# Queries and keys laid out in DRAM by head and half of the tokens: shorter rows, eight stores a group

## What is computed

```
x = x + attn_b(layernorm(x), w_qkv, w_o)

def attn_b(x, w_qkv, w_o):             # b = 16, s = 1024, hid = 256, heads = 16, d = 16
    qkv = x @ w_qkv.T * hid ** -0.5
    q, k, v = split by head            # each (b, heads, s, d)
    attn = softmax(q k^T * d ** -0.5) * (s / sqrt(s - 1))
    out = attn v * s ** -0.5
    return out @ w_o.T * hid ** -0.5
```

## Time and profile before

| what | value |
|---|---|
| median of 3 runs | 5751.51 us (5750.79 to 5752.28) |
| the profiled execution, its own time | 5750.62 us |
| its span in the profile | 5748.9 us |
| mean granted TensorE clock | 0.976 of full |
| TensorE (PE) busy | 5428.0 us, 94% of the span |
| VectorE (DVE) busy | 4498.2 us, 78% |
| ScalarE (ACT) busy | 3566.0 us, 62% |
| GpSimd (POOL) busy | 1473.5 us, 26% |
| DMA packets | 317697, 512.58 MB, mean 89 GB/s |

### The profile page before, as it was taken

One profiled execution on the slowest core, in us unless ns is written; L12 is line 12 of the kernel. 1 busy time (PEld: TensorE's weight loads), 2 busy tenths in 40 slices (PEclk: granted clock), 3 DMA queues, 4 the chain that ended last, 5 costly groups with the idle time before them and its releaser, 6 DMA issues. The chain is left out here.

```text
span 5748.9 us, 131254 instructions
## 1 busy us (share of the span) xinstructions
PE 5428.0 (94%) x50092; PEld 3660.4 (64%) x50092; DVE 4498.2 (78%) x7377; ACT 3566.0 (62%) x5406; POOL 1473.5 (26%) x1948
## 2 busy tenths in 40 slices
PE   7999668999989889999999999999999997799999
PEld 6777457999978734444444444444444444699998
DVE  7888695555557689999999999999999996755554
ACT  5777562333325458888888888888888886433332
POOL 4655453333310000111111111111111114533332
PEclk9999889999999989999999999999999998999999
DMA  2222482222229811121112111111211113222221
GB/s 74 78 84 78 137 259 77 88 93 93 89 96 333 310 56 49 58 60 57 57 59 60 57 56 60 59 57 56 60 58 57 57 54 104 75 89 93 95 86 49
DMA packets 317697, 512.58 MB, mean 89 GB/s; under 512 B 36442, under 2 KB 221156, under 8 KB 311152
## 3 DMA queue, kind: packets, MB, share of 16 engines
q1 hardware_dynamic: 291912, 441.44, 24.2%
q0 software_dynamic: 24576, 64.56, 3.5%
q10 hardware_dynamic: 808, 1.07, 0.1%
HBM read 338.59 MB, written 185.60 MB: 91 GB/s over the span
## 5 line engine op out<-in xcount | busy, mean ns | idle before, releaser
L1773 DVE TENSOR_REDUCE at_best<-at_psM 128x2 f32<-128x1024 f32 x2048 | 2430.7, 1221 | 227.5 <-PE at_psM L1830 214.3
L1729 ACT ACTIVATE at_p<-at_psE 128x1024 f32<-128x1024 f32 (+1 forms) x2688 | 2077.1, 824 | 529.5 <-PE at_psE L1846 515.7
L1846 PE MATMUL at_psE<-at_q,at_k 50*128 50x512 f32 x4096 | 1174.0, 436 | 7.5 <-ACT at_p L1729 6.3
L1830 PE MATMUL at_psM<-at_k,at_q 48*128 48x512 f32 x4096 | 1093.6, 458 | 37.5 <-DMA at_k<-scratch_qk 27.4
L1857 PE MATMUL at_psO<-at_p,at_v 128*17 128x256 f32 x16384 | 1109.9, 383 | 0.1
L1122 ACT ACTIVATE e_h_hi<-e_psH 128x512 fp32r<-128x512 f32 x512 | 306.7, 599 | 916.0 <-PE e_psH L90 864.4
L1846 PEld LDWEIGHTS at_psE<-at_q,at_k 50*128 50x128 f32 x4096 | 548.7, 185 | 462.4 <-issue 223.6
L1196 DVE SCALAR_TENSOR_TENSOR e_h_lo<-e_psH,e_h_hi 128x512 fp32r<-128x512 f32 x512 | 353.9, 691 | 595.9 <-ACT e_h_hi L1122 505.8
L1857 PEld LDWEIGHTS at_psO<-at_p,at_v 128*17 128x17 f32 x16384 | 364.1, 96 | 542.7 <-issue 345.4
L1830 PEld LDWEIGHTS at_psM<-at_k,at_q 48*128 48x128 f32 x4096 | 471.3, 185 | 312.2 <-DVE at_best L1773 147.2
L90 PE MATMUL e_psE<-e_w_hi,e_h_hi 128*128 128x256 f32 x2048 | 583.1, 285 | 0.0
(11 more groups left out here) (213 smaller groups left out, 8456.5 us busy)
## 6 DMA issues: line engine op xcount, KB each, us to landing
e_w_raw<-in_w SPq DMA_DIRECT2D x64, 1024.0 KB
scratch_qk<-cp_qkh SPq DMA_DIRECT2D x64, 512.0 KB
scratch_qk<-cp_qkl SPq DMA_DIRECT2D x64, 512.0 KB
at_q<-scratch_qk SPq DMA_DIRECT2D x256, 128.0 KB
at_k<-scratch_qk SPq DMA_DIRECT2D x252, 128.0 KB
scratch_v<-cp_va SPq DMA_DIRECT2D x32, 544.0 KB
at_v<-scratch_v SPq DMA_DIRECT2D x126, 136.0 KB, 10.0
a_x<-in_x SPq DMA_DIRECT2D x32, 512.0 KB
```

The lines of the kernel that those rows point to most:

```text
L1729: nc.scalar.activation(P[:, u:u + n, :], src, ACT.Exp, scale=HD ** -0.5).then_inc(p_ready, 1)
L1773: nc.vector.reduce_max(best[j % 2][:, h, :, qt], psM[h][:], AX_X).then_inc(m_taken, 1)
L1830: last = nc.tensor.matmul(psM[h][:, a, :], Q[j][r, 128 * qt:128 * qt + 128], K[j][r, 512 * h:512 * h + 512], start=True, stop=True)
L1846: last = nc.tensor.matmul(psE[:, u - u0 if n == 2 else 2, :], K[j][r, 128 * kc:128 * kc + 128], Q[j][r, 512 * half:512 * half + 512], star ...
```

## The change

`qk` becomes [256, 2, 4, 16, 512]: head of a batch, half of the tokens, part, feature, token of the half. The row of one head, half and feature is now 2 KB long. A load of 32 or 16 rows takes each row of its tile as two pieces of 2 KB, one from each half, and high and low parts lie next to each other, so that part and feature are one dimension. A store takes one chunk: 128 partitions of the tile go to 8 heads x 16 features. That makes eight DMAs of 256 KB a group where there were four of 512 KB, and the counts on qkv_stored go from 80 to 144 (nine DMAs of 16). Bytes, buffers and all arithmetic stay as they are.

```diff
-    qkb = qk.rearrange("r (b h) d n -> b r (h d) n", h=H)
+    qkb = qk.rearrange("(b c h) s r d n -> s b c r h d n", c=2, h=H // 2)
...
             def store_qkv(g, s, i):
-                half = slice(G * s, G * s + G)
                 sp.wait_ge(qk_lo_ready, 4 * g + 4)
                 for part in range(2):
-                    cs = slice(2 * part, 2 * part + 2)
                     for r, buf in ((2 * part, QKH), (2 * part + 1, QKL)):
-                        sp.dma_start(row(qkb, i)[r, :, half].rearrange("(c p) n -> p c n", p=128), buf[s][:, cs, :].bitcast(F32)).then_inc(qkv_stored[s], 16)
+                        for c in range(2):
+                            sp.dma_start(row(qkb[s], i)[c, r], buf[s][:, 2 * part + c, :].bitcast(F32)).then_inc(qkv_stored[s], 16)
...
             for s in range(2):
-                sp.wait_ge(qkv_stored[s], 80 * (NG // 2))
+                sp.wait_ge(qkv_stored[s], 144 * (NG // 2))
...
             def group(g, s, i):
-                after(act, qkv_stored[s], 80 * i)
+                after(act, qkv_stored[s], 144 * i)
...
-    qkp = qk.rearrange("r (u x) d n -> u x r d n", x=2)
+    qkp = qk.rearrange("(u a) s r d n -> u a (r d) s n", a=2)
...
             for a in range(2):
                 r = 64 * a
-                eng.dma_start(Q[j][r:r + 32, :].bitcast(F32), row(qkp, pp)[a, 0:2]).then_inc(qk_loaded[j], 16)
-                eng.dma_start(Q[j][r + 32:r + 48, :].bitcast(F32), row(qkp, pp)[a, 0]).then_inc(qk_loaded[j], 16)
+                eng.dma_start(Q[j][r:r + 32, :].bitcast(F32), row(qkp, pp)[a, 0:32]).then_inc(qk_loaded[j], 16)
+                eng.dma_start(Q[j][r + 32:r + 48, :].bitcast(F32), row(qkp, pp)[a, 0:16]).then_inc(qk_loaded[j], 16)
...
-                eng.dma_start(K[j][r:r + 16, :].bitcast(F32), row(qkp, pp)[a, 2]).then_inc(qk_loaded[j], 16)
-                eng.dma_start(K[j][r + 16:r + 48, :].bitcast(F32), row(qkp, pp)[a, 2:4]).then_inc(qk_loaded[j], 16)
+                eng.dma_start(K[j][r:r + 16, :].bitcast(F32), row(qkp, pp)[a, 32:48]).then_inc(qk_loaded[j], 16)
+                eng.dma_start(K[j][r + 16:r + 48, :].bitcast(F32), row(qkp, pp)[a, 32:64]).then_inc(qk_loaded[j], 16)
...
-    qk, v = scratch("qk", [4, NH, 16, S]), scratch("v", [N // S, 128, 2, H, 4, 17])
+    qk, v = scratch("qk", [NH, 2, 4, 16, S // 2]), scratch("v", [N // S, 128, 2, H, 4, 17])
```

## The result

The changed kernel takes 5880.45 us (median of 6 runs, 5873.81 to 5893.97), the kernel before 5751.55 us (6 runs). The ratio is **1.0224**, 95% interval 1.0208 to 1.0239: slower by 2.2%. The profiled execution took 5873.81 us with a span of 5872.1 us, 123.2 us more than the span before.

What follows compares the result with a forecast made beforehand. TensorE bounds projection and attention before; the change makes eight DMA engines bound the projection. Stage +150 and attention head -13 give +137 us on the profiled 5750.6: 5887.6, plus 0.9 to the median, 5888 us; range 5840 to 5940.

Steps and rivals of the forecast that it cites:

- The width of a DMA follows its outermost dimension: All DMAs: engines used follow the outermost dimension, up to 16; changed stores get 8 engines, changed loads 16.
- third sign: Sign of DMA width: issuing a load with 2 or 8 outermost takes 671 and 680 ns, with 16 takes 412.
- The stage, +150 us: Projection, first query store to first query load: 14.3 us a group on eight loaded engines, 454 us instead of 304.3.
- the 384 GB/s of the old drain: Last stores alone on 16 engines, 24.0 GB/s each; so 192 on eight, 10.9 us for a group's query and key stores.
- Shares of the stage: Projection stage after the change: 222 GB/s, a DMA share of about 0.55, TensorE busy two thirds.
- Who waits: Projection: ScalarE waits for stores of two groups back, VectorE for ScalarE, TensorE for VectorE; SP's issuing, 0.68 us a store, hidden.
- The head, -13 us: Head of the attention: wider loads of pair 0 let TensorE's first product start 13 us earlier; bounds 8 and 15.5 us.
- The middle of the attention, 0: Middle of the attention: faster loads stay hidden by three pairs of lead, no TensorE wait on a DMA; counted 0.
- The sum: Whole kernel: +150 - 13 = +137 us on 5750.6 gives 5887.6; median 0.9 us above the profiled execution, so 5888 us.
- Stores that aren't narrowed: Rival in the projection: stores spread over 16 engines or take turns, stage stays at 9.5 us a group, 5738 us; 8%.
- The clock: Rival in the projection: TensorE's pauses drop its clock to 1.2 GHz for good, 19 us a group, 6042 us; 4%.
- Something more behind narrow stores: Rival in the projection: distant heads or gaps between small stores slow the eight engines, 17 us a group, 5973 us; 6%.

Runs made afterwards that it cites:

- wide_stores: Changed kernel with feature outside and head inside a chunk's partitions, so its eight stores are 16 x 8 x 512; 5751.41 us, 0.9997 of the kernel before.
- stores_4_wide: Changed kernel with sixteen stores of 128 KB a group, each 4 x 16 x 512, instead of eight; 6176.85 us in one run.
- values_twice: Changed kernel with each group's values stored a second time, to a tensor that nobody reads; 5948.43 us in one run.
- wide_loads_only: Kernel before, stores and layout untouched, each load of 2 x 16 rows split into two of 16; 5743.61 us, 0.9986 of the kernel before.

## Why the prediction was right, point by point

The direction, the mechanism and the place were right; 5880 us lies in 5840 to 5940 and 8 us under the 5888 predicted. The terms one by one:

- **The width of a DMA follows its outermost dimension.** Read from the short packets before the change, it held after it: 96 a group and 208 a pair in the changed kernel, 160 a group in wide_stores, and 2755 for 28.7 groups, 96, in stores_4_wide. (8x8, 16x4 and 4x16 are all 64, so the 96 says something only beside the number of stores.) The Trainium skill's rule (DMA: Bandwidth & Descriptors, "Why a DMA increments its semaphore by 16 and not by 1") agrees with all of these. That the same engines are used again, the drain of stores_4_wide shows; the rates go with the width, 102 GB/s at 4 wide and 204 at 8 wide. The prediction's third sign, issue time, doesn't hold in general: the 16 x 8 stores of wide_stores run on 16 engines and took 545 ns at the least, 580 in the median, to issue.
- **The stage, +150 us.** Measured +136. The group takes 440.3 / 32 = 13.8 us and not 14.3. Query and key stores alone run at 204 GB/s on eight engines, not 192: they take 10.3 us, next to the 10.2 that I had as the lower bound. An engine among eight is a little faster than among sixteen (25.5 against 24.0 GB/s). Values and x then hold 3.5 us, where I had 3.4; values_twice puts 2.2 of them on the values. The choice of the 384 GB/s of the old drain for the rate per engine is the term that was mis-sized: 10.9 us a group for stores that take 10.3. With the 0.1 us more for values and x that is 0.5 us a group, 16 us in 32 groups, and 14 were missing.
- **Shares of the stage.** 230 GB/s inside the stage against the 222 forecast, but a DMA share of 0.65 and not 0.55. Here the forecast had left something out: by its own terms the eight engines without stores work 3.4 of 14.3 us on values and x, which makes the mean 0.62.
- **Who waits.** ScalarE at the first chunk, 101.7 us in 29 waits, behind it VectorE and TensorE, as forecast. SP's issuing was hidden, though a store took 1.08 us to issue and not 0.68.
- **The head, -13 us.** Measured -12.4. wide_loads_only shows that the width of the loads alone does it.
- **The middle of the attention, 0.** Measured: 3.8 us of TensorE's waits in 2590 us, all on ScalarE, where there were 4.4 in 2600:

```profile
PE at_psE L1845 <- ACT at_p L1728: 3.8, 6, 0.6
```

- **The sum.** +136 - 12.4 on 5750.6 is 5874.3, and the profiled execution took 5873.8. It is at the low end of six runs that lie 20 us apart; the median is 6.6 us higher, where I had expected 0.9. So it is partly luck that the total came within 8 us: against the profiled execution, for which the sum was made, the forecast of 5887.6 is 14 us too high.
- **The rivals.** Stores that aren't narrowed: excluded by the packets, the 204 GB/s and stores_4_wide. The clock: it did fall, to 0.87 in the mean of the stage. Two groups of the changed kernel in two windows, and TensorE at the first chunk that waited:

```profile
1806.80:1827.40 20.60, 16.04 (x89) 13.97 (x88) 10.82 (x29) 6.96 (x11) 0.00 (x0) 0.83 0.70 241
1827.40:1834.20 6.80, 5.77 (x30) 4.41 (x29) 3.30 (x8) 2.61 (x6) 0.00 (x0) 1.00 0.52 199
```

```profile
1818.45 0.80 PE L90 MATMUL cp_psQ<-cp_xhi,cp_w_hi 128*128 128x512 f32 x1 [4.56 <-DVE cp_qkl L1429]
1819.04 0.63 PE L90 MATMUL cp_psQ<-cp_xlo,cp_w_hi 128*128 128x512 f32 x1
```

  After 4.56 us without work a matmul of 512 columns took 0.63 us instead of 0.39, for part of the group. This is at least part of why TensorE's busy share was 0.80 and not two thirds. As forecast, the slack took it up: with less work for TensorE the stage got no shorter. Something more behind narrow stores: 13.8 us a group, so no.

## What to carry to other kernels

Look at the outermost dimension of both sides of a DMA before its size: in all these kernels it set how many of the 16 engines carried it, and a layout that no longer lets two dimensions merge can halve the rate of a store whose bytes and rows look as good as ever. The number of packets under 512 B per DMA told the width in these traces. A narrow load that lies behind other work costs nothing until a stage begins with it; two loads of 16 rows in place of one of 2 x 16 got the gain of this change without its price.

## What the runs showed of the hardware that was not expected

- Stores of 16 x 8 rows use 16 engines and are still slower than stores of 128 rows: 324 or 325 GB/s at a share of 0.97 against 333 at 0.95, in three layouts. The number of stores made no difference (304.8 against 304.3 us), nor did 4 KB between the heads (313.2 against 313.8).
- A DMA on all 16 engines that is issued behind narrow stores starts at once on the engines that are free: in the drain of stores_4_wide twelve sixteenths of the values moved while stores issued before them still ran on the other four.
- The six runs of the changed kernel lie 20 us apart. That the DMA bound makes the time less steady isn't shown: the kernel before has sets of 6 to 23 runs that lie 12 to 20 us apart.
